# A fused attention kernel: in the last four slots of the cross attention, TensorE sums the softmax denominators chunk by chunk and GpSimd subtracts the maximum from the odd chunks

## What is computed

```python
q = (query @ wq.T + bq).reshape(B, SQ, H, HD).transpose(0, 2, 1, 3)
k = (key @ wk.T + bk).reshape(B, -1, H, HD).transpose(0, 2, 1, 3)
v = (value @ wv.T + bv).reshape(B, -1, H, HD).transpose(0, 2, 1, 3)
scores = jnp.einsum('bhqd,bhkd->bhqk', q, k) / jnp.sqrt(jnp.asarray(HD, q.dtype))
attn = jax.nn.softmax(scores, axis=-1)
ctx = jnp.einsum('bhqk,bhkd->bhqd', attn, v)
return ctx.transpose(0, 2, 1, 3).reshape(B, SQ, D) @ wo.T + bo
```

## Time and profile before

| what | us |
|---|---|
| median of the runs (3 runs, 1859.74 to 1862.59) | 1859.81 |
| the profiled execution | 1860.6 |
| its span, from the first to the last instruction | 1858.2 |
| cross attention with projections beside it, in the span | about 55 to 1137 |
| its end without projections (last slots) | about 1137 to 1247.4 |
| the stages behind it | 1248 to 1858 |

### The profile page before, as it was taken

One profiled execution on the slowest core, in us unless ns is written; L12 is line 12 of the kernel. 1 busy time (PEld: TensorE's weight loads), 2 busy tenths in 40 slices (PEclk: granted clock), 3 DMA queues, 4 the chain that ended last, 5 costly groups with the idle time before them and its releaser, 6 DMA issues. The chain is left out here.

```text
span 1858.2 us, 36962 instructions
## 1 busy us (share of the span) xinstructions
PE 1716.2 (92%) x15305; PEld 1377.4 (74%) x15320; DVE 1224.5 (66%) x1631; ACT 962.7 (52%) x1470; POOL 776.3 (42%) x343
## 2 busy tenths in 40 slices
PE   6899999999999999999999997538999689879999
PEld 5688888888888888888888875437887466658886
DVE  5126887887887787787787788957332677753223
ACT  2236666666666666666666665533220677731000
POOL 0002555555555555555555555662000466622210
PEclk9999999999999999999999998658999899989999
DMA  4211111111111111110110102103650533201101
GB/s 162 69 46 38 38 29 40 38 28 40 38 30 38 38 34 34 38 40 28 38 41 27 38 7 71 44 29 131 201 179 14 159 92 90 68 24 46 45 23 45
DMA packets 104189, 104.94 MB, mean 56 GB/s; under 512 B 7263, under 2 KB 72799, under 8 KB 104044
## 3 DMA queue, kind: packets, MB, share of 16 engines
q1 hardware_dynamic: 104044, 102.83, 18.2%
HBM read 79.74 MB, written 23.07 MB: 55 GB/s over the span
## 5 line engine op out<-in xcount | busy, mean ns | idle before, releaser
L517 POOL TENSOR_TENSOR b_acc<-b_acc,b_s 128x1024 f32<-128x1024 f32 x192 | 525.7, 2738 | 294.6 <-ACT b_s L705 282.3
L733 DVE TENSOR_TENSOR b_s<-b_s,b_mb 128x2048 f32<-128x2048 f32 x128 | 372.5, 2912 | 15.7 <-ACT b_mb L692 15.7
L762 DVE TENSOR_TENSOR b_mx<-b_psS,b_mx 128x512 f32<-128x512 f32 x480 | 331.1, 690 | 44.2 <-PE b_psS L587 31.1
L705 ACT ACTIVATE b_s<-b_s 128x2048 f32<-128x2048 f32 x128 | 245.1, 1915 | 89.3 <-DVE b_s L733 89.3
L713 ACT ACTIVATE b_s<-b_psS 128x2048 f32<-128x2048 f32 x128 | 241.1, 1884 | 50.8 <-DVE b_mx L762 50.4
L43 PE MATMUL b_work<-cT,wkT 128*128 128x512 f32 x512 | 211.0, 412 | 0.0
L43 PE MATMUL b_work<-wvT,cT 128*128 128x512 f32 x512 | 209.4, 409 | 0.0
L512 POOL TENSOR_TENSOR b_acc<-b_s 128x1024 f32<-128x1024 f32 x32 | 80.8, 2525 | 290.8 <-PE b_psO L611 179.8
L44 PE MATMUL b_work<-cT,wkT 128*128 128x512 f32 x512 | 201.0, 393 | 0.0
L45 PE MATMUL b_work<-cT,wkT 128*128 128x512 f32 x512 | 200.7, 392 | 0.0
L45 PE MATMUL b_work<-wvT,cT 128*128 128x512 f32 x512 | 200.2, 391 | 0.0
(11 more groups left out here) (221 smaller groups left out, 3036.7 us busy)
## 6 DMA issues: line engine op xcount, KB each, us to landing
cin<-in_ctx SPq DMA_DIRECT2D x64, 512.0 KB, 3.7
q_scratch<-d_st SPq DMA_DIRECT2D x32, 256.0 KB, 2.5
k_scratch<-d_st SPq DMA_DIRECT2D x32, 256.0 KB, 2.5
e_q<-q_scratch SPq DMA_DIRECT2D x16, 512.0 KB, 3.5
k_sb<-k_scratch SPq DMA_DIRECT2D x64, 128.0 KB, 3.6
experts_sb<-in_L_ffn_expert_w SPq DMA_DIRECT2D x8, 1024.0 KB, 5.2
x_sb<-in_x SPq DMA_DIRECT2D x2, 1024.0 KB, 7.1
q_scratch<-a_q SPq DMA_DIRECT2D x4, 512.0 KB, 3.2
```

Of the source, the lines that this page charges most:

```text
L517: nc.gpsimd.tensor_tensor(acc[:, :, :], acc[:, :, :], s[:, buf, 2 * i:2 * i + 2, :], ALU.add).then_inc(sum_done, 1)
L705: nc.scalar.activation(part, part, ACT.Exp, scale=SCALE).then_inc(exp_done, 1)
L733: nc.vector.tensor_tensor(s[:, n % BUFS, :, :], s[:, n % BUFS, :, :], mb[:, :].rearrange("p (o n) -> p o n", o=1).broadcast_to([P, CHUNK, ...
L762: nc.vector.tensor_tensor(mx[:, :, :], part, mx[:, :, :], ALU.max).then_inc(mx_done, 1)
```

## The change

All of it holds from slot `TAIL` = 28 on (the last four slots, chunks 112 to 127); the slots ahead run as before.

1. GpSimd makes no sums there. Instead TensorE multiplies the tile of ones with each chunk of exponentials right behind that chunk's value matmuls (`chunk_denominators`, 16 matmuls each, accumulated over the slot in columns 0 to 127 of bank `work2`). The increment of `pv_done` moves to the last of them. The reciprocal waits for `pv_done` of the slot's last chunk and reads `work2`.
2. GpSimd subtracts `mb` from the odd chunks, in two instructions of 128 x 1024 each (`pool_sub_done`); VectorE does the even chunks only. The exponentials, and the copy to `mb` of the next slot, wait for the counts of both.
3. From beat 256 the ring of turned maxima uses two banks instead of three.
4. A score buffer is free with `pv_done` alone there.

```diff
+        TAIL = SLOTS - 4
+        def on_pool(n):
+            return n // CHUNK >= TAIL and n % 2 == 1
...
+        def enter(unit, beat):
+            banks = BANKS if beat < SLOTS * SLOT else BANKS - 1
...
             for n in range(SLOTS * CHUNK):
                 m, c = divmod(n, CHUNK)
                 buf = n % BUFS
+                if m >= TAIL:
+                    if on_pool(n):
+                        pool.wait_ge(s_moved, n + 1)
+                        pool.wait_ge(mb_done, m + 1)
+                        for i in range(2):
+                            nc.gpsimd.tensor_tensor(
+                                s[:, buf, 2 * i:2 * i + 2, :], s[:, buf, 2 * i:2 * i + 2, :],
+                                mb[:, :].rearrange("p (o n) -> p o n", o=1).broadcast_to([P, 2, HG * P]),
+                                ALU.subtract).then_inc(pool_sub_done, 1)
+                    continue
...
+                if m >= TAIL:
+                    last = chunk_denominators(n)
                 last.then_inc(pv_done, 1)
+
+            def chunk_denominators(n):
+                c = n % CHUNK
+                if n == TAIL * CHUNK:
+                    wait_evicted(after[BANKS - 1])
+                for i in range(CHUNK):
+                    for j in range(HG):
+                        last = nc.tensor.matmul(work[BANKS - 1][j * HD:(j + 1) * HD, 0:P], ones[:, :],
+                                                s[:, n % BUFS, i, j * P:(j + 1) * P],
+                                                start=c == 0 and i == 0, stop=c == CHUNK - 1 and i == CHUNK - 1)
+                return last
...
-                if (m := sum_slot(beat)) is not None:
+                if (m := sum_slot(beat)) is not None and m < TAIL:
                     denominators(m)
...
-                    reached(act, sub_done, m * CHUNK)
+                    reached(act, sub_done, vector_subs(m * CHUNK))
+                    reached(act, pool_sub_done, pool_subs(m * CHUNK))
...
-                    act.wait_ge(sub_done, n + 1)
+                    if on_pool(n):
+                        act.wait_ge(pool_sub_done, pool_subs(n + 1))
+                    else:
+                        act.wait_ge(sub_done, vector_subs(n + 1))
...
-                        act.wait_ge(sum_done, sums_of(n - BUFS))
+                        if (n - BUFS) // CHUNK < TAIL:
+                            act.wait_ge(sum_done, sums_of(n - BUFS))
...
-                if (n := exp_step(beat)) is not None:
+                if (n := exp_step(beat)) is not None and not on_pool(n):
...
-                    dve.wait_ge(od_full, m + 1)
-                    nc.vector.reciprocal(rD[:, :], psO[:, P:2 * P]).then_inc(rd_done, 1)
+                    if m < TAIL:
+                        dve.wait_ge(od_full, m + 1)
+                    else:
+                        dve.wait_ge(pv_done, (m + 1) * CHUNK)
+                    sums = psO[:, P:2 * P] if m < TAIL else work[BANKS - 1][:, 0:P]
+                    nc.vector.reciprocal(rD[:, :], sums).then_inc(rd_done, 1)
```

More of the change, by code:

```diff
@@ L334, in cross_attention, with pool_subs, vector_subs @@
         MAXIMA = CHUNK * CHUNK
+        TAIL = SLOTS - 4
+        def on_pool(n):
+            return n // CHUNK >= TAIL and n % 2 == 1
+        def pool_subs(n):
+            return 2 * max(0, n // 2 - TAIL * CHUNK // 2)
+        def vector_subs(n):
+            return n - pool_subs(n) // 2
         def steps(beat, first, every, count):
@@ L437, in cross_attention @@
         sub_done = sem("b_sub_done")
+        pool_sub_done = sem("b_pool_sub_done")
         exp_done = sem("b_exp_done")
@@ L527, in _, with wait_evicted @@
             pe.wait_ge(const, 1)
[L529 to L532, removed]
+            def wait_evicted(unit):
+                if unit is not None:
+                    kind, m, n = unit
                     if kind == "T":
@@ L542, in bank_of @@
                         pe.wait_ge(mb_done, m + 1)
-                return work[i % BANKS]
+            def bank_of(unit):
+                wait_evicted(LAST_IN[unit])
+                return work[BANK[unit]]
             def transposes(p, n):
@@ L657, in _ @@
                     if u < CHUNK:
-                        i = RING["K", p, u]
+                        i, bank = RING["K", p, u], work[BANK["K", p, u]]
                         act.wait_ge(work_full, i + 1)
@@ L663, in _ @@
                         at = key_place(b, u, c)
-                        nc.scalar.activation(kT[:, at:at + 512], work[i % BANKS][:, :], ACT.Identity,
+                        nc.scalar.activation(kT[:, at:at + 512], bank[:, :], ACT.Identity,
                                              bias=bk[:, u:u + 1]).then_inc(k_done, 1)
@@ L667, in _ @@
                         u -= CHUNK
-                        i = RING["V", p, u]
+                        i, bank = RING["V", p, u], work[BANK["V", p, u]]
                         act.wait_ge(work_full, i + 1)
@@ L675, in _ @@
                         if step == P:
-                            nc.scalar.activation(v[:, at[0]:at[0] + D], work[i % BANKS][:, :],
+                            nc.scalar.activation(v[:, at[0]:at[0] + D], bank[:, :],
                                                  ACT.Copy).then_inc(v_done, 1)
@@ L721, in _ @@
                 if (m := spread_slot(beat)) is not None:
-                    i = RING["M", m, 0]
+                    i, bank = RING["M", m, 0], work[BANK["M", m, 0]]
                     dve.wait_ge(work_full, i + 1)
                     reached(dve, spread_done, m - 1)
-                    nc.vector.tensor_reduce(top[:, m % 2, :], work[i % BANKS][:, :].rearrange("p (j k) -> p j k", j=HG),
+                    nc.vector.tensor_reduce(top[:, m % 2, :], bank[:, :].rearrange("p (j k) -> p j k", j=HG),
                                             AX.X, ALU.max).then_inc(top_done, 1)
-                if (n := exp_step(beat)) is not None:
+                if (n := exp_step(beat)) is not None and not on_pool(n):
                     m, c = divmod(n, CHUNK)
@@ L751, in _ @@
                     dve.wait_ge(hi_done, p * CHUNK + n + 1)
-                    nc.vector.tensor_tensor(context_place(cT[1], p, n), two(work[RING["T", p, n] % BANKS]),
+                    nc.vector.tensor_tensor(context_place(cT[1], p, n), two(work[BANK["T", p, n]]),
                                             f32(context_place(cT[0], p, n)), ALU.subtract).then_inc(split_done, 1)
```

26 lines of the change are left out of this document (15 added, 11 removed).

## The result

The changed kernel takes 1839.8 us in the median (four runs, 1836.5 to 1843.3), against 1860.9 beside it: a ratio of 0.9886, with a 95% interval of 0.9865 to 0.9908. Two more comparisons gave 0.9876 and 0.9891. Over its 13 runs it took 1838.8 in the mean with a standard deviation of 2.9, and the kernel before 1859.5 over 33 runs with 2.1. In each of the three comparisons by itself the means lie 21.2, 22.5 and 20.7 us apart. So the gain is 21.5 us, give or take 2; 16.3 had been forecast, and 1843.5 as the time. The profiled execution of the changed kernel was its slowest of the first four, 1843.3, with a span of 1841.5.

A forecast was written before the change was run, and what follows sets the result against it. The prediction took the score chain, VectorE and GpSimd taking turns, and the closing chain to bound the kernel's end. Gains 8.2 + 3.1 + 5.0 = 16.3 us gave 1843.5 us, range 1836 to 1851.

The forecast's parts named there:

- the score chain: Last slots: one PSUM score tile makes scores, maxima and move follow each other, 7.06 us a group, 28.2 for four.
- the engines taking turns: Last slots: VectorE and GpSimd alternate rather than share; a VectorE subtraction takes 2.28 us alone, 4.31 beside GpSimd's additions.
- the closing chain: End of stage: the reciprocal waits for GpSimd's late additions, 13.19 us after the last exponential's start.
- Term A: Closing chain: denominators on TensorE replace GpSimd's queue, 13.19 us becoming 4.2 to 5.9; gain taken as 8.2.
- Term B: Slot 31's subtractions, divided between VectorE and GpSimd taking turns: 14.3 us instead of 17.4, gain 3.1.
- The forecast's aside: Slot 31: taking the engines as parallel would give 9.4 us for its four chunks, gain 8.0, total 1838.6.
- Term C: Slots 28 to 30: slots of 28.3 us instead of 30.3, gain 5.0; bounds 14.7 gained or 7.0 lost, by clock.
- the 0.6 to 0.85 that had been named: Sign for the last slots: a mean TensorE clock outside this range would show the slots 28 to 30 estimate wrong.
- Nothing was hidden: Answers a rival: the end of this stage doesn't set the next, gain hidden by a load, 1860 us; chance 0.05.
- nothing is gained or lost there: Behind the stage: everything after the barrier starts earlier by the same amount, loads still issued with ample time.
- GpSimd as the bound: Rival, last slots: GpSimd's subtractions at 4.35 us each and TensorE at the lower clock give 1864 us; chance 0.05.
- TensorE as the bound: Rival, last slots: TensorE stays at 1.2 GHz and becomes the bound, 3.4 us gained, 1857; chance 0.07.

The follow-up runs named there:

- part 1 alone: The changed kernel with all subtractions back on VectorE; TensorE's denominators, two-bank ring and buffers freed by `pv_done` stay: 1834.7 us mean, stage 103.16.
- part 2 alone: The kernel before, with GpSimd subtracting from odd chunks besides its sums; denominators and three-bank ring as before: 1861.8 us mean, ratio 1.0015, stage 127.56.
- the denominators twice: The changed kernel with each denominator matmul of the last four slots issued twice into the same sums: 1841.0 us mean, stage 109.35.

## Why the prediction was right

**What bounds the end.** The reading held in the main: the score chain, the engines taking turns, the closing chain. In the first profile the three terms were, measured against forecast, A 9.13 (8.2), B 3.66 (3.1), C 5.99 (5.0): 18.8 in all for 16.3. All three came out larger than forecast, so no error hid another; but a part of term C came from a place that the forecast had not looked at.

**Term A.** Right in mechanism. The middle of the two clocks was too careful: the last two groups took 1.08 us each, the rate of the higher clock, and the chain 4.06, below the forecast's 4.2. TensorE had worked without a pause from 1219.13 to 1224.5 and its rate had risen within that run; before the change the last value products, 2.42 us of waiting ahead of them, took 1.94. That the doubled work is what lifted the clock was not tested by itself.

**Term B.** Right, and its premises with it. GpSimd's subtraction with the repeated `mb` has a minimum of 2341 and a median of 2370 ns, VectorE's a minimum of 2281 (changed kernel, 1133 to 1240):

```profile
L535 POOL TENSOR_TENSOR b_s<-b_s,b_mb x15: 2341/2370/4466, 1131.9 to 1221.4; 128x1024 f32<-128x1024 f32 x15
L786 DVE TENSOR_TENSOR b_s<-b_s,b_mb x7: 2281/2292/4473, 1139.4 to 1214.7; 128x2048 f32<-128x2048 f32 x7
```

The queue of both was through in 13.7 us for the 14.3 summed. What the forecast did not ask is what part 1 gives without part 2. It counted the 3.1 as a gain of the change; the run of part 1 alone makes it 6.8, so part 2 took 3.1 away. The sentence that the two engines take turns was there, with the prices 4.72 and 2.28; from it follows that where nothing but subtractions is left to do, as in slot 31, splitting them loses. The forecast's aside, that someone who took the engines as parallel would expect 1838.6, happens to name the mean that was measured, 1838.8: that is chance, since the parallel engines would need 9.4 us in slot 31, and it was 13.7.

**Term C.** The direction and nearly the size were right; slots of 28.5 and 28.3 us stand for the 28.3 taken, and 6.0 us for the 5.0. But 28.3 was chosen between 25.4 and 33.8 and not worked out, so that it came within 0.2 us is luck, and only a third of the 6.0 comes from the score chain. Reckoned from the end of the turn ahead of each copy (L619, L667 after) instead of from the copy, slots 28 to 30 took 29.4, 30.5 and 28.5 us before and 29.5, 28.5 and 28.3 after: 2.1 us gained, nearly all in slot 29. The other 3.9 are the copy of slot 31 alone. These are the lines ahead of it in the kernel before:

```profile
1208.49 4.31 DVE L733 TENSOR_TENSOR b_s<-b_s,b_mb 128x2048 f32<-128x2048 f32 x1
1209.64 1.12 PE L619 MATMUL b_work<-ident,b_spread 128*128 128x128 f32 x4
1212.84 1.91 ACT L705 ACTIVATE b_s<-b_s 128x2048 f32<-128x2048 f32 x1 [3.60 <-DVE b_s L733]
```

and this one in the changed kernel:

```profile
1208.36 1.12 PE L667 MATMUL b_work<-ident,b_spread 128*128 128x128 f32 x4
```

The turn ends at 1210.76, and the copy starts at 1214.65, since ScalarE has the exponential of slot 30's last chunk ahead of it, which waits for a subtraction that a turn of GpSimd lengthened to 4.31. After the change GpSimd has done that chunk long before, and the copy starts 0.03 us behind the end of its turn, at 1209.51. The copies of slots 29 and 30 were 2.2 and 2.0 us late in the same way. That is the 2.1 us measured in slot 28, where 1.0 was taken: its chain gave nothing. The forecast has no step for this wait. With part 1 alone the copy of slot 31 is 1.0 us behind its turn and with part 2 alone 1.7, so either part removes more than half of it. That is one reason why 6.7 and 5.0 us in the slots do not add up, both parts giving 6.0.

In the chain itself the reason given, VectorE late for the maxima, holds with others beside it. From score group to score group slot 29 has 7.89, 7.06, 7.29 and 7.98 us before, and 6.82, 6.15, 7.82 and 8.30 after. The scores took 1.8 us less in all by the higher clock, and VectorE was 1.3 us less late for the maxima. Against it, value products and new denominators ahead of the next slot's scores cost 1.2 us more, and the move at 1169.08 waited 0.7 us for the denominators of an older chunk that still held its buffer; the forecast had put that at nothing.

**The clock.** The mean over 1122 to 1230 is 0.81, inside the 0.6 to 0.85 that had been named; before the change the same window had 0.65.

**Behind the stage.** Nothing was hidden: the next stage starts 0.79 us behind VectorE's last instruction, as before. But the step "nothing is gained or lost there" holds only on the average. The stages behind took 612.0, 608.5 and 608.6 us in three profiles of the changed kernel, against 610.8 in the one of before; over the profiles of all kernels that leave these stages as they are, it was 604.6 to 612.0. That the mean gain is 21.5 and the stage gives 18.8 leaves 2.7 us, which lie within this spread and are not explained further.

**The rivals.** GpSimd as the bound came true in part 2 alone (+2.7 us in the stage), where it also carries the sums. TensorE as the bound did not for the slots as a whole, even with the denominators twice. Two figures of the forecast are off: 3.4 us off 1859.8 is 1856.4 and not 1857, and with the lower clock's terms GpSimd's price makes the change slower from about 3.2 us an instruction, not 4.3. Neither bears on the result. Faster, with its chance of 0.87, came true.

## What to carry to other kernels

Before giving half of an elementwise job to GpSimd, look in the timeline at an instruction of VectorE with two SBUF inputs that runs beside it: if it takes its own time plus GpSimd's, the two take turns, and the move replaces a cheap turn by a dear one. A change with two parts should be priced by part; here one part brought 21.7 to 22.5 us of stage time, and adding the other lost 2.9 to 4.2. Where a slot is measured from an instruction that can itself be late, look at what it waits for before giving the gain to the chain ahead of it. In a stretch where TensorE is half idle, sums over partitions can be cheap on it (256 matmuls more cost 3.3 us here), and where they stand in its order was worth 2.3 to 5.2 us.

## What the runs showed of the hardware

- VectorE's subtractions with two inputs in SBUF and GpSimd's instructions took turns one by one: 2.28 us alone against 4.47 behind one of GpSimd's. Maxima with one input in PSUM kept their 0.7 us.
- Work of GpSimd that nobody waits for lengthened the stage by 4.2 us.
- GpSimd's instruction of 128 x 1024 with both inputs and the output in the same tile took 1.9 us, with two tiles 2.36.
- 256 more matmuls cost the stage 3.3 us, the mean granted clock of the window going from 0.81 to 0.89.
- Two profiles of one kernel, equal up to 1262 us, differed by 3.4 us in span, with clocks of 0.82 and 0.94 in the same window of 28 us.
